# Self-attention stages of a two-layer perceiver on one core: the causal mask added by TensorE, row maxima read straight from PSUM, a score buffer per token tile, and value products behind the first scores

## The reference, cut to what matters

```python
qkv = (x @ qkv_w + qkv_b).reshape(b, s, 3, h, hd)          # 16 heads of 32
logits = jnp.einsum('bqhd,bkhd->bhqk', q, k)
causal_mask = jnp.triu(jnp.ones((s, s), bool), 1)
logits = jnp.where(causal_mask, -jnp.inf, logits) * scale
att = jax.nn.softmax(logits, axis=-1)
out = jnp.einsum('bhqk,bkhd->bqhd', att, v).reshape(b, s, d)
return out @ out_w + out_b
```

## Time and profile before

| what | value |
| --- | --- |
| time, median of 3 runs | 2594.85 us (2593.65 to 2602.11) |
| the profiled execution | 2598.24 us, of which its span of instructions is 2596.5 us |
| stage `b`, first normalisation to next stage's first instruction on DVE | 929.12 to 1034.83 us: 105.7 us |
| stage `e`, likewise | 2120.18 to 2222.62 us: 102.4 us |
| busy share of the span: PE, DVE, ACT, POOL | 86%, 40%, 28%, 16% |
| mean granted TensorE clock | 0.923 of full speed |

### The profile page before, as it was taken

The page is one execution under the profiler, slowest core; times in us unless marked ns, Lnnn a source line. Parts: engine busy times, 40 slices in busy tenths (PEclk is TensorE's granted clock), DMA queues, the critical chain, the costliest instruction groups (busy, mean ns, idle before and its releaser), DMA issues. The chain is left out here.

```text
span 2596.5 us, 26998 instructions
## 1 busy us (share of the span) xinstructions
PE 2236.0 (86%) x10194; PEld 1341.1 (52%) x10194; DVE 1044.8 (40%) x2135; ACT 735.0 (28%) x1462; POOL 421.4 (16%) x477
## 2 busy tenths in 40 slices
PE   5799999999999885799999878776898966599996
PEld 2355555555555433444444435444454434499996
DVE  4345655655655025200000258777294035422110
ACT  2334544544444112211111143342153101111111
POOL 0000000000000000489993111222000000000001
PEclk8999999999999997799999988776899987799998
DMA  5001222122121220868877364231400010556552
GB/s 193 26 15 47 72 74 64 52 75 75 41 70 54 93 73 21 315 261 315 314 309 282 131 212 134 95 114 39 171 33 16 0 66 2 218 210 242 218 207 92
DMA packets 131539, 327.33 MB, mean 126 GB/s; under 512 B 39857, under 2 KB 89170, under 8 KB 111827
## 3 DMA queue, kind: packets, MB, share of 16 engines
q1 hardware_dynamic: 99392, 297.20, 31.7%
q10 hardware_dynamic: 29202, 19.49, 2.4%
q0 software_dynamic: 2816, 8.92, 1.0%
HBM read 303.22 MB, written 21.24 MB: 125 GB/s over the span
## 5 line engine op out<-in xcount | busy, mean ns | idle before, releaser
L868 PE MATMUL a_mix<-a_xn,a_probs_T 128*128 128x384 f32 (+1 forms) x832 | 313.4, 493 | 14.3 <-issue 10.2
L797 PE MATMUL a_sc<-a_wk_centred,a_ctx_T 128*128 128x512 f32 x624 | 288.3, 599 | 4.3 <-DVE a_keys L462 2.3
L1774 PE MATMUL c_gate_up<-c_w_wide,c_h_rows 128*128 128x512 f32 x480 | 210.9, 592 | 0.0
L868 PEld LDWEIGHTS a_mix<-a_xn,a_probs_T 128*128 128x128 f32 (+1 forms) x832 | 145.5, 191 | 119.8 <-issue 72.3
L797 PEld LDWEIGHTS a_sc<-a_wk_centred,a_ctx_T 128*128 128x128 f32 x624 | 117.9, 192 | 129.2 <-issue 106.0
L1679 DVE TENSOR_TENSOR c_hidden<-c_silu,c_gate_up 128x512 f32<-128x512 f32 x38 | 26.1, 688 | 355.1 <-PE c_gate_up L1774 343.3
L2198 PE MATMUL f_ring<-f_picked_T,f_w 128*128 128x160 f32 x1024 | 146.6, 304 | 1.0 <-DVE f_picked_T L2039 1.0
L1774 PEld LDWEIGHTS c_gate_up<-c_w_wide,c_h_rows 128*128 128x128 f32 x480 | 90.1, 190 | 108.1 <-issue 108.1
L462 DVE SCALAR_TENSOR_TENSOR a_keys<-a_k_bias,a_std,a_sc 128x512 f32<-128x512 f32 (+1 forms) x104 | 77.1, 742 | 167.6 <-PE a_sc L797 167.6
L2198 PEld LDWEIGHTS f_ring<-f_picked_T,f_w 128*128 128x128 f32 x1024 | 142.9, 193 | 1.3 <-DVE f_picked_T L2039 1.1
L2213 PE MATMUL f_ring<-f_hidden,f_w 128*128 128x160 f32 x1024 | 141.2, 300 | 0.4 <-ACT f_hidden L2100 0.4
(11 more groups left out here) (489 smaller groups left out, 3505.6 us busy)
## 6 DMA issues: line engine op xcount, KB each, us to landing
c_w_wide<-in_L_ffn_W SPq DMA_DIRECT2D x68, 1024.0 KB, 7.0
f_w<-in_L_ffn_W SPq DMA_DIRECT2D x32, 2048.0 KB, 9.5
c_w_down<-in_L_ffn_W SPq DMA_DIRECT2D x34, 1024.0 KB, 7.5
a_ctx_T<-in_ctx_T SPq DMA_DIRECT2D x48, 384.0 KB, 3.6
a_xn<-in_ctx SPq DMA_DIRECT2D x24, 768.0 KB, 6.4
d_context_T<-in_ctx_T SPq DMA_DIRECT2D x24, 768.0 KB, 10.5
d_context<-in_ctx SPq DMA_DIRECT2D x8, 2304.0 KB
mixed_context<-a_mixed_T ACTq DMA_DIRECT2D x84, 64.0 KB, 1.8
```

The costliest lines, as they stand in the source:

```text
L797: last = pe.matmul(key_bank(b, t), ctx_T[:, n % AHEAD, k, cols], wk_centred[:, k, :], start=(k == 0), stop=(k == KC - 1))
L868: ins = pe.matmul(mix[:, 0:DC], probs_T[0:m, t, p * P:(p + 1) * P], xn[0:m, b % 2, t, :], start=(t == 0), stop=(t == CT - 1))
L1774: last = pe.matmul(gate_up[2 * (u % 2) + part][:], h[:, k, :], w_wide[:, i % WIDE_RING, k, :], start=(k == 0), stop=(k == KD - 1))
```

## The change

All of it is in `causal_attention`, and both stages use it.

- **Mask by TensorE.** POOL fills two tensors of 128 x 512, `picked` (ones where the row picks a query position) and `hidden` (-1e30 where the key is later than the query), and ACT turns each into bf16 rows (8 small copies). `pair_scores` then begins with 16 bf16 products of 512 columns (two halves h, two batches b, four row groups i) that lay the mask into PSUM, and the score products add to it (`start=False`).
- **Maxima from PSUM.** `centre` has no mask additions; the maximum and the subtraction each read all four banks in one instruction. The second pair of scores waits for `centred` (the subtraction) where it waited for `masked`.
- **A score buffer per token tile.** `scores`, `top` and `total` have NT slots; the wait of centre(2) and centre(3) for the transposes is gone.
- **Order in stage `b`.** PE makes the scores of pair 0 right after queries and keys, then value products 0 and 1, the scores of pair 1, value products 2 and 3. DVE's order is written out anew. `v_ready` is still raised after the last value tile. In stage `e` the order stays, but PE's wait for `ring_out` at `R_TILE` now stands behind the scores.

```diff
-        scores = s.sb("scores", [P, 2, H, SEQ])
+        scores = s.sb("scores", [P, NT, H, SEQ])
...
-            for t in range(NT):
+            def put_values(t):
                 u = R_V + t
                 dve.wait_ge(ring_full, u + 1)
...
-            dve.sem_inc(v_ready, 1)
-            dve.wait_ge(mask_made, 4)
+                if t == NT - 1:
+                    dve.sem_inc(v_ready, 1)

             def centre(t):
-                if t >= 2:
-
-                    dve.wait_ge(ring_full, R_TILE + 4 * (t - 2) + 2)

                 dve.wait_ge(scores_full, t // 2 + 1)
-                for i in range(4):
-                    dve.tensor_tensor(scores[:, t % 2, 4 * i:4 * i + 4, :], bank[i][:, t % 2, :, :],
-                                      causal[:].unsqueeze(1).to_broadcast([P, 4, SEQ]), ALU.add).then_inc(masked, 1)
-                dve.wait_ge(masked, 4 * t + 4)
-                own.did(dve.tensor_reduce(top[:, t % 2, :], scores[:, t % 2, :, :], AXX, ALU.max))
-                own.wait()
-                dve.tensor_tensor(scores[:, t % 2, :, :], scores[:, t % 2, :, :],
-                                  top[:, t % 2, :].unsqueeze(2).to_broadcast([P, H, SEQ]),
-                                  ALU.subtract).then_inc(centred, 1)
+                mine = bank[:, :, t % 2, :, :]
+                own.did(dve.tensor_reduce(top[:, t, :].rearrange("p (i c) -> p i c", i=4), mine, AXX, ALU.max))
+                own.wait()
+                dve.tensor_tensor(scores[:, t, :, :].rearrange("p (i c) k -> p i c k", i=4), mine,
+                                  top[:, t, :].rearrange("p (i c) -> p i c", i=4).unsqueeze(3)
+                                  .to_broadcast([P, 4, 4, SEQ]), ALU.subtract).then_inc(centred, 1)
...
             def pair_scores(pair):
                 if pair >= 1:
-                    pe.wait_ge(masked, 8 * pair)
+                    pe.wait_ge(centred, 2 * pair)
+                for h in range(2):
+                    for b in range(2):
+                        for i in range(4):
+                            r = slice(HD * i, HD * i + HD)
+                            pe.matmul(bank[b * SEQ:b * SEQ + SEQ, i].rearrange("p t c k -> p (t c) k"),
+                                      pick_row[r, h, :], mask_row[r, h, :].unsqueeze(1).to_broadcast([HD, 8, SEQ]),
+                                      start=(h == 0), stop=False, skip_group_check=True)
...
-                                last = pe.matmul(bank[i][rows_b, t % 2, c, :], qk_T[r, c, tok], qk_T[r, key, tok],
-                                                 start=True, stop=True)
+                                last = pe.matmul(bank[rows_b, i, t % 2, c, :], qk_T[r, c, tok], qk_T[r, key, tok],
+                                                 start=False, stop=True, skip_group_check=True)
...
+            pe.wait_ge(ring_out, R_TILE)
             for t in range(NT):
                 pe.wait_ge(probs_ready, t + 1)
```

More of the change, by code:

```diff
@@ L1224, in divide @@
                                   ALU.mult).then_inc(probs_ready, 1)
-            centre(0)
[L1227 to L1230, removed]
+            if rope:
+                for t in range(NT):
+                    put_values(t)
+                centre(0)
+                for t in range(NT):
+                    if t + 1 < NT:
+                        centre(t + 1)
+                    divide(t)
+            else:
+                centre(0)
+                centre(1)
+                divide(0)
+                put_values(0)
+                divide(1)
+                put_values(1)
+                centre(2)
+                put_values(2)
+                centre(3)
+                put_values(3)
+                divide(2)
+                divide(3)
@@ L1285, in _, with values @@
                 last.then_inc(ring_full, 1)
-            for t in range(NT):
+            def values(t):
                 u = R_V + t
@@ L1309, in pair_scores, with ready @@
                                 r = slice(HD * i, HD * i + HD)
[L1310 to L1311 removed]
+                                last = pe.matmul(bank[rows_b, i, t % 2, c, :], qk_T[r, c, tok], qk_T[r, key, tok],
+                                                 start=False, stop=True, skip_group_check=True)
                 last.then_inc(scores_full, 1)
[L1314 to L1315 removed]
+            def ready():
+                if rope:
+                    pe.wait_ge(heads_ready, NQK)
+                else:
+                    pe.wait_ge(ring_out, R_V)
+                pe.wait_ge(rows_made, 8)
+            if rope:
+                for t in range(NT):
+                    values(t)
+                ready()
+                pair_scores(0)
+                pair_scores(1)
+            else:
+                ready()
+                pair_scores(0)
+                values(0)
+                values(1)
+                pair_scores(1)
+                values(2)
+                values(3)
+            pe.wait_ge(ring_out, R_TILE)
             for t in range(NT):
```

54 lines of the change are left out of this document (28 added, 26 removed).

## The result

The changed kernel took 2582.91 us (median of 10 runs, 2578.02 to 2588.31), the kernel before in the same series 2594.25 us (10 runs, 2590.33 to 2607.78). The ratio is 0.9948, with a 95% interval of 0.9930 to 0.9967: faster by 0.5%. By the ratio that is 13.5 us, by the medians 11.3 us, against 19.1 us forecast. The forecast median was 2576 us with an own range of 2571.5 to 2580.5; 2582.91 lies above that range and inside the whole one, 2567 to 2587.

A forecast was written before the change was run, and what follows sets the result against it. Bound: the chain inside stages b and e, PE until the projections end, then DVE with its waits. Savings of 8.9 us (e) and 10.2 us (b) make 19.1; 2594.85 less that gives 2576 us, range 2567 to 2587.

The forecast's parts named there:

- own range: Whole program: the interval given to the main forecast of 2576 us, 2571.5 to 2580.5 us, chance 0.54.
- the two waits for a buffer: DVE, before centre(2) and centre(3): waits of 2.06 us each for transposes to free score buffers, 4.1 us in stage e.
- rival 2: New PE and PSUM work is dearer than its rows: 5 to 10 us less gain, 2581 to 2586 us; chance 0.18.
- three dearer terms: Stages b and e: mask products in fewer rounds, 0.2 us on each PSUM read, slow clock in first output products.
- Centre: DVE, per token tile: 3.84 us before, of which 1.45 us of mask additions are removed and 2.39 us stay.
- PSUM reads without surcharge: DVE reduction and subtraction in centre: an operand in PSUM costs nothing extra; other bound 0.2 us per instruction.
- 62 cycles: DVE instructions with a PSUM source: the skill's extra over SBUF, making the sum about 0.5 us smaller; not used.
- Mask products: PE, ahead of each pair's scores: 16 products in two rounds, 0.45 us at full clock, 0.9 us at half.
- Rival 4: PE score products lose overlap when adding to PSUM: 38 us more against 19 saved, 2614 us; chance 0.05.
- the wait for the value copies: PE at the start of stage e: this wait is gone, up to 0.3 us, not counted in the sum.
- The wait for the transfer: PE in stage b: the value part of tile 0 waits for v_swapped, delaying what is queued behind by about 3.4 us.
- Rival 1: Clock stays at 2.4 GHz through the tiles in b, e or both: about 5 us more gain, 2571 us; chance 0.14.

The follow-up runs named there:

- e1: The kernel before the change, run again with no edit; 0.9992 of its own time, median 2601.04 us.
- e2: The changed kernel run again with no edit; 0.9936 of the time of the kernel before, median 2579.81 us.
- e3: The changed kernel with the mask added on DVE again and maxima read from SBUF; stage b 100.2 us, stage e 97.5 us, one profile.
- e6: e5 plus the old wait of centre(2) and centre(3) for the transposes, as with two score buffers; b 103.1 us, e 98.4 us, one profile.
- e7: e4 with all four exponentials of stage b ahead of ACT's tile copies; b 93.6 us, 0.9917 of the time of the kernel before.
- e9: The same program as e7, run again; stage b 88.0 us, 0.9936 of the time of the kernel before.
- e4: The changed kernel with v_swapped moved per token tile, one semaphore each; stage b 89.8 us, 0.9929 of the time of the kernel before.
- e5: The changed kernel with the old order in stage b, all value products ahead of the first scores; b 94.9 us, e 94.1 us, one profile.
- e10: e7 with four unused transposes ahead of each value part (in stage e, tiles 2 and 3); b 86.7 us, 0.9899 of the kernel before.

## Why the prediction was right, and where it was not

- **Sign and place: right.** The gain is in `b` and `e`; 19.1 us forecast, 20.0 in the first pair of profiles, 20.7 in e1 against e2. The mask's removal and the two waits for a buffer each did their part (e3, e6).
- **The total: too large a gain.** The step that failed is the sum's silent one, that the untouched stages stay as they are in the profiled execution and in the median. Stage `a` moved by 7.4 us between two executions, and the timed runs carried 13.5 us in one series and 16.6 in the other (by the ratios, 0.0064 x 2601; by the medians 11.3 and 21.2). The forecast's own margin of 4.5 us either way came from its terms alone; the 7 to 8 us of stage `a` weren't in it. The prediction did name this very picture, changed stages shorter by 19 us while another stage has become longer, as a sign of being wrong. That 2582.91 lies in the band of rival 2 (2581 to 2586) is chance: none of the three dearer terms of rival 2 is in the changed kernel's trace. In stage `d` the changed kernel had 635.5 and 635.6 us against 633.1 and 633.2; e7 and e9, one program, had 633.0 and 636.7, so this need not be the change's doing, but it isn't settled. How the remaining difference of the medians divides among stages can't be read from executions without a profile.
- **Prices: right.** Centre 2.39 us forecast, 2.40 measured. PSUM reads without surcharge: a reduction takes 1.21 us from either side. The 62 cycles of the Trainium skill (VectorE: DVE Perf Modes, TRN2 errata) don't show in these rows. Mask products 0.45 us per pair at 2.4 GHz, as forecast, and 0.85 at 1.2 GHz against 0.9 (2174.01 - 2173.16). Rival 4, scores that lose their overlap, has fallen: 1.54 and 2.21 us, not 6.9 and 13.8.
- **Stage e: the chain right, its start wrong.** Counted from the first centre, pair 1 was forecast at 4.9 us, centre(2) at 8.2, tile 3 at 22.5; measured 4.93, 8.03, 22.35. But the first centre came 50.0 us into the stage, not 51.0. PE began the pair 0.43 us earlier (47.87 us into the stage against 48.30), because the wait for the value copies, which the prediction named and didn't count, is gone. And from the first score to the first centre it was 1.68 us against 2.28: in the profile of before the 128 score instructions come in two pieces with a break, 113 of them in 1.46 us and then 15 more, where after they took 1.61 us in one piece. The second piece:

```profile
2170.22 0.37 PE L1310 MATMUL e_bank<-e_qk_T 32*64 32x64 f32 x15 [0.28 <-issue]
```

In e1, the same program as before, they came in one piece of 1.64 us and the centre 1.81 us after the first score, so 0.5 of the 0.6 us is a chance of the one profile from which the price was read. Together with the 0.43 us that is 1.0 of the 1.3 us by which the stage beat its forecast.
- **Stage b: right, with one term too small.** No gap on DVE for 18.1 us (18.2 forecast), value part of tile 0 held by the DMA, exp(2) behind it. The wait for the transfer was 5.2 us, not 3.4. One half of the difference is the start of the value part behind the landing: the engines' share fell 5.85 us after `v_ready`, just as it did before (5.9), but PE went on 1.3 us after that, where the prediction had allowed 0.2. The other half is that the first transposes ran at 2.4 GHz (1.09 us where I had 1.97), so that the copies were ready 0.8 us earlier; this half costs nothing in the chain. Tile 3 started 75.9 us into the stage against 75.6 forecast. For this transfer the Trainium skill (DMA: Bandwidth & Descriptors) would give 4.4 us, an estimate; the trace has 5.85 us until the share falls and 7.16 until PE goes on.
- **That this late transfer gives something back** was shown by e4: 5.3 us of the chain. The prediction called it 3.4 us of wait and didn't see that it comes near the whole worth of moving the value products: with the late transfer, the new order of `b` shows no gain over the old one (e5).
- **Rival 1, a full clock through the tiles,** didn't happen in the changed kernel; in e2 the clock was up from the value part of tile 2 on, and `b` was 0.8 us shorter than after. e10, with other edits, has a full clock throughout, and `b` is 1.2 to 6.8 us shorter than in e9 and e7, the same program without the added transposes; the rival had about 5 us for `b` and `e`. **Rival 2's** late clock rise showed in e6, e7 and `e` of e9 instead, worth 2 to 4 us each, in the output product.

## What to carry to other kernels

When work is moved ahead of a step that signals a DMA, the signal moves too: send the data in the pieces in which they become ready, and wait for each piece where it is used (5 to 6 us of a 96 us stage here). Where VectorE bounds the chain and TensorE waits, an addition that can be a product into the same PSUM bank is nearly free: here 1.45 us of DVE work per tile for 0.22 us of PE at 2.4 GHz, or 0.43 at 1.2 GHz. Before a forecast of a few microseconds is put on a 2.6 ms program, look how far its untouched stages move from one execution to the next, and give the range at least that much.

## What the hardware showed beyond expectation

- Untouched stage `a` ran in 928.2 to 929.9 or in 936.5 to 937.1 us and nothing between in 13 profiles; granted clock from 40 to 80 us 0.96 in every short one and 0.81 to 0.83 in every long one.
- One and the same program (e7, e9) ran its output product's first 5 us at 0.50 in one execution and from its start at 1.00 in the other; the stage took 93.6 and 88.0 us.
- Four transposes of 128 columns (0.60 us) put into each gap of some 0.7 us between transposes and value part went with a clock of 1.00 through all tiles of `b` in both kernels that had them, one profile each.
- Two transfers of 512 KB each from SBUF to SBUF kept the DMA engines busy until 5.9 us after the last value tile was out, before and after alike. The engine that waited for them went on only 1.3 us after that (after: 1001.0 and 1002.31), 7.2 us after that tile in after, e2 and e3.
